# Products of zeros ahead of the maximum products of two sequences, and a plan drawn anew, in an attention and mixture-of-experts layer

## Time and profile before

| | |
|---|---|
| runs, us | 601.95, 604.53, 609.40; median 604.53 |
| the profiled execution | 607.28 us, of which the span from the first to the last instruction is 605.5 |
| mean granted clock of TensorE over the span | 0.933 |
| PE matmuls busy | 534.6 us (88%), 4350 instructions |
| DVE busy | 487.4 us (80%), 1981 instructions |
| ACT, POOL busy | 313.4 us (52%), 309.5 us (51%) |
| HBM | 64.28 MB read, 20.05 MB written |

### The profile page before, as it was taken

One profiled execution on the slowest core, in us unless ns is written; L12 is line 12 of the kernel. 1 busy time (PEld: TensorE's weight loads), 2 busy tenths in 40 slices (PEclk: granted clock), 3 DMA queues, 4 the chain that ended last, 5 costly groups with the idle time before them and its releaser, 6 DMA issues.

```text
span 605.5 us, 14722 instructions
## 1 busy us (share of the span) xinstructions
PE 534.6 (88%) x4350; PEld 355.4 (59%) x4350; DVE 487.4 (80%) x1981; ACT 313.4 (52%) x744; POOL 309.5 (51%) x517
## 2 busy tenths in 40 slices
PE   6869898979999899999999999999996977899841
PEld 3222354535656556656657777666876977885431
DVE  3797998968999889899899879879942774758883
ACT  3106945645756556567666655776661442432100
POOL 5215826555363456667874556547584423143531
PEclk9776997989999989999999899999997997999986
DMA  6483332173535445453675375643455698860111
GB/s 187 124 255 94 94 116 68 54 227 124 129 86 162 112 149 154 140 153 110 182 191 145 106 225 157 182 124 111 120 169 185 181 291 266 259 197 23 48 39 36
DMA packets 75279, 87.40 MB, mean 144 GB/s; under 512 B 9984, under 2 KB 57984, under 8 KB 75200
## 3 DMA queue, kind: packets, MB, share of 16 engines
q1 hardware_dynamic: 67984, 77.34, 43.7%
q0 software_dynamic: 3584, 7.35, 4.1%
q10 hardware_dynamic: 3632, 1.77, 1.0%
HBM read 64.28 MB, written 20.05 MB: 139 GB/s over the span
## 4 chain that ended last, share of the span: by engine, by line
PE 57%; DVE 14%; issue 10%; SPq 6%; ACT 5%; DMA 3%; another core or an unknown queue 2%; POOL 1%; ACTq 0%; DVEq 0%
PE ps L1462 15%; PE ps L1368 10%; PE ps L1324 10%; PE ps L1474 8%; DVE sums L1581 3%; PE ps L1379 3%; ACT probs L1169 2%; PE ps L1446 2%; SPq L960 2%; PE ps L1310 2%; PE ps L1484 1%; PE ps L1395 1%; DVE acc L1761 1%; PE ps L1410 1%
## 5 line engine op out<-in xcount | busy, mean ns | idle before, releaser
L1581 DVE CUSTOM_DVE_ANT_0 sums<-ps,mask_sb 128x384 bf16<-128x384 f32 (+3 forms) x512 | 218.0, 483 | 14.5 <-PE ps L1324 10.8
L1169 ACT ACTIVATE probs<-ps 128x512 f32<-128x512 f32 x320 | 170.9, 612 | 50.3 <-PE ps L1324 46.5
L1103 POOL TENSOR_SCALAR_AFFINE_SELECT probs<-probs 128x256 f32<-128x256 f32 (+1 forms) x320 | 114.2, 365 | 126.6 <-ACT probs L1169 118.8
L1324 PE MATMUL ps<-stack 64*128 64x256 bf16 (+3 forms) x1024 | 118.3, 314 | 14.5 <-DMA stack<-mparts 5.7
L1462 PE MATMUL ps<-xgT,w_tile 128*128 128x128 f32 x672 | 92.3, 284 | 3.6 <-ACT xgT L1230 2.8
L1462 PEld LDWEIGHTS ps<-xgT,w_tile 128*128 128x128 f32 x672 | 83.3, 197 | 10.7 <-issue 6.8
L1713 DVE SCALAR_TENSOR_TENSOR gate<-th,ps 128x256 f32<-128x256 f32 x116 | 48.5, 418 | 46.9 <-ACT th L1236 39.5
L1125 POOL DMA_INDIRECT yg<-rows_out,slot x56 | 54.0, 964 | 60.4 <-DVE acc L1761 33.9
L1368 PE MATMUL ps<-probs,va 128*32 128x512 f32 (+3 forms) x1024 | 81.0, 459 | 3.6 <-POOL probs L1103 1.4
L1324 PEld LDWEIGHTS ps<-stack 64*128 64x128 bf16 x1024 | 41.8, 95 | 71.5 <-issue 16.7
L1236 ACT ACTIVATE th<-ps 128x256 f32<-128x256 f32 x116 | 45.1, 390 | 52.2 <-PE ps L1462 36.6
(11 more groups left out here) (119 smaller groups left out, 707.6 us busy)
## 6 DMA issues: line engine op xcount, KB each, us to landing
w_tile<-in_experts SPq DMA_DIRECT2D x92, 384.0 KB
stack<-parts_scratch SPq DMA_DIRECT2D x98, 128.0 KB
parts_scratch<-parts SPq DMA_DIRECT2D x14, 384.0 KB
xg<-rows_in SPq DMA_DIRECT2D x18, 256.0 KB
rows_out<-y_routed SPq DMA_DIRECT2D x61, 64.0 KB
rows_in<-zeros SPq DMA_DIRECT2D x14, 192.0 KB, 3.7
x_t<-in_x SPq DMA_DIRECT2D x8, 256.0 KB
x_r<-in_x SPq DMA_DIRECT2D x8, 256.0 KB
```

The costliest lines, as they stand in the source:

```text
L1103: pool.affine_select(out=area, in_=area, compare_op=ALU.is_ge, fill=0.0, base=0, pattern=pattern, channel_multiplier=-1).then_inc(masked, 1)
L1169: act.activation(probs[:, (s * NB + v) % PRING, :], bank("scores", s, v), ACT.Exp, scale=SCALE)\
L1324: return pe.matmul(into[:, at:at + width], here[:, stationary, at_s:at_s + P], here[:, moving, at_m:at_m + width], start=True, stop=True)
L1581: ins = dve.tensor_tensor_reduce(sums[:, use % 2, at:at + w], bank("max", s, u)[:, at:at + w], mask_sb[:, S - w:S], -1.0, 3.0e38, ALU.add, ...
```

## The change

1. `max_pair`, for sequences 0 and 1: the waits for the two banks of a pair both come first; then come two rounds of products of `idle`, in each round one on rows 0 to 63 into the first bank and one on rows 64 to 127 into the second, 128 by 512; then the products of before, which overwrite the zeros. Sequences 2 to 7 issue the same instructions as before, apart from the two waits, which come first there too.
2. `length`: in the plan a pair of these two sequences takes 430 ns more.
3. All numbers in `AT` and `LATER` are drawn anew; the code that uses them is the same, and so is `COST`. "Searched under drawn delays" in the change's name says that the search for the numbers went through plans with random delays drawn into them.

```diff
-AT = dict(weight_ahead=110.3736, tables=5.4067, fill=-93.4985, fill_step=26.5143, routed0=9.7812, routed1=-2.4771,
+AT = dict(weight_ahead=76.186, tables=-17.3658, fill=-124.8669, fill_step=32.6219, routed0=9.1224, routed1=0.5053,
...
-         ("pe", "max_pair"): (-172.1, -167.21, -5.43, -127.49, -148.68, -100.62, -14.13, -12.09, -100.6, -237.59,
-         169.06, -18.79),
+         ("pe", "max_pair"): (-177.61, -128.53, 37.43, -74.99, -88.61, -59.18, 33.94, 18.05, -62.24, -216.71, 216.99,
+         -13.08),
...
+
+WARMED, WARMING = 2, 2
...
+        if kind == "max_pair" and key[0] < WARMED:
+            taken, lasts = taken + 215 * WARMING, lasts + 215 * WARMING
...
                 for pair in range(2):
                     take("max", s, 2 * w + pair)
+                for _ in range(WARMING if s < WARMED else 0):
+                    for pair in range(2):
+                        zero = idle[KS * pair:KS * pair + KS, :]
+                        pe.matmul(bank("max", s, 2 * w + pair), zero[:, 0:P], zero, start=True, stop=True)
+                for pair in range(2):
                     for k, i, at in MAX_UNITS[b]:
```

More of the change, by code:

```diff
@@ new lines @@
+AT = dict(weight_ahead=76.186, tables=-17.3658, fill=-124.8669, fill_step=32.6219, routed0=9.1224, routed1=0.5053,
+          routed2=137.2347, stay=0.5386, values=-3.6375, v=29.1374, rows1=3.9149, maxima1=-70.4109, heads_T0=-10.8792,
+          heads_T1=-180.518, out_T=38.1973, out=-125.2214, ln1_stats=23.0964, ln1=-8.2064, x1_T=46.1952,
+          router=36.0633, weights=70.8658, load_residual=69.3691, load_x=-50.3811, x_T=-71.6631, project0=-44.8146,
+          project1=-79.1125, rope=53.9864, rest=79.4813, low=-67.116, store_parts=-132.8503, stack0=-75.8479,
+          stack1=-51.451, rows0=-8.3374, maxima0=-76.2422, count=-15.9543, rank=-61.6646, scatter=128.7884,
+          scatter_step=0.115, shared=27.7133, shared_step=2.72, routed=48.9194, margin=2.3458, apart=1.2735,
+          T=-2.8221, tanh=21.694, glu=1.5347, down=-61.4607, stored=-120.3842, weight_late=14.1817, gather=-2.1911,
+          gather_step=0.7016, combine=51.1716, lull_from=-58.3092, lull_to=18.6836, lull=1.2261,
+          routed_last_but_one=1.6586, routed_last=8.7267, apart_last=0.756, gather_last=114.7465,
+          gather_step_last=1.0571, combine_last=-6.6777, dense=-1.8198, dense_step=1.3239, dense_tanh=40.0325,
+          dense_glu=98.9924, dense_down=83.4753, dense_mix=-41.9754, dense_weight=-69.8979, dense_weight_step=19.6751)
```

253 lines of the change are left out of this document (109 added, 144 removed), and 31 rows, old and new, of the table LATER.

## The result

The kernel after takes 627.12 us (median of 4 runs, 624.62 to 629.50) where the kernel before took 606.68 beside it: 1.0335 of its time, with a 95% interval of 1.0278 to 1.0392, 20.4 us more. The forecast was 599.0 us with a range up to 613. It was wrong, in the sign as well. The profiled execution of after took 629.50 us, of which the span is 627.8.

A forecast was written before the change was run, and what follows sets the result against it. DVE was taken to bound 21.2 to 44.7 us, PE at low clock 44.7 to 57, and PE's work 150 to 455. Terms 0 - 2 + 2 + 0.5 - 2 - 4 = -5.5 us gave 599.0 us against the median; range 587 to 613.

The forecast's parts named there:

- f: New places of all instructions on five queues: -4 us taken, bounded by 23.1 us of PE's idle time either way.
- Price of a round: Two added products of zeros on PE, side by side: 0.22 us at full clock; two rounds 0.44 full, 0.89 half.
- a: 21.2 to 44.7 us, DVE full: 15 pairs' zeros, 6.6 us, fit PE's 7.0 us idle, so 0; +6.4 if clock low.
- b: 44.7 to 57 us: higher clock saves 4.2 us, five pairs' zeros cost 2.2, so -2; bounds -5.6 to +4.4.
- c: 57 to 78 us, clock already 1.00: 13 pairs' zeros, 5.7 us, against 2.26 us idle PE; +2, bounds 0 to +3.4.
- d: 78 to 96.5 us: seven pairs' zeros, 3.1 us, against 2.6 us idle PE; +0.5, bounds 0 to +3.1.
- the 4 us named: Sign: the fourth transpose of maxima still stands near 96 us, within 4 us.
- e: Low-clock stretches at 97.8, 118.3 and 135.3 us, which no zeros reach: -2 us from re-placed work, bounds -8.4 to +3.4.
- D: Rival, 0.14: zeros come to about nothing; the new order moves 455 to 560 us by up to 13.2 us; 590 to 616.
- C: Rival, 0.14: zeros lengthen the path of sequences 0 and 1 on PE's queue, 21 to 96 us: +14.7, 619.2 us.
- B: Rival, 0.22: zeros keep the clock full in 43.2 to 56.8 us and three later stretches: -18.0, 586.5 us.

## Why the prediction was wrong

**The failed step is f.** The prediction put it so: "The long stretch is 97% busy, which leaves order little, so I take a sixth, -4." The order alone measures +2.7% (the kernel without zeros), 16.6 us by its ratio to the 604.53 us of the runs before the prediction, some 20 us from that -4. The bound of 23.1 us, "as much the other way", held; the choice near nothing failed. What the step left out is the wait: with indirect DMAs 1.27 us apart the other engines learned up to 15.3 us late that PE had finished, and spacing them takes 3.9 points off after, more than the 3.35 that the change cost. The argument was that a stretch with little idle time has little to lose. It has little to win; a stretch that is 97% busy can lose any amount, and from 150 to 455 us PE's idle time grew by 12.6 us, over the 8 us that the prediction had named as a sign against f. I had asked how good the new order could be for PE and not what it does to POOL's queue, though "past POOL's gathers too" stood in the step.

**The evidence was at hand.** The chain and the waits were read at the start of the kernel, since most of the low clock was there. ACT's idle time of 7.78 us with no known releaser, in the middle of nine scatters, was in the trace of before, and the chain of before has 2% of "another core or an unknown queue" with one core. The code shows it as well: `plan` keeps a least distance between indirect DMAs (`GAP, GAP_LAST, GAP_END = 2600, 1300, 0`, L225), and lets PE's work end at least 1.1 us after an indirect DMA that was issued less than 1 us before that end (`HOLD`, L226 and L724). It reads as if the late signals had been known, though no comment says so. But the distance is kept in the plan's time only. The queue that comes out of it holds scatter after scatter with nothing between, and once POOL is late they can start as fast as it issues them, 1.27 us apart. For the last group the plan even allows 1.3 us, which is no more than that pace, and takes it that PE's work comes through between two of them; the traces show that for most of a run it does not.

**The terms, one by one.**
- Price of a round, 0.22 us: right (0.44 and 0.85 us for two), though the ratio of 1.9 that I named gives 0.23. The Trainium skill (TensorE: Matmul & The Clock Gate, Part 3, "The mechanism") has weight loads run under a matmul in flight only where the row groups differ, which would have each round show its weight load; the two rounds of 0.44 us do not bear that out here either. The same section also names loads into a background weight buffer, with which 0.44 us would agree; no run here tells whether that is the way.
- a, 0: right. DVE is busy 23.12 of 23.50 us, and in the order of before the first transpose of maxima stood at 37.7 us (38.03 in the earlier trace rows).
- b, -2: right for the clock, not for the time. The first values group fell from 4.49 us to the 2.36 that was forecast; with the same order and no zeros it takes 4.21. PE of after, then of the new order without zeros:

```profile
52.78 2.36 PE L1372 MATMUL ps<-probs,va 128*32 128x512 f32 x32
...
51.69 4.21 PE L1372 MATMUL ps<-probs,va 128*32 128x512 f32 x32 [0.51 <-POOL probs L1102]
```

But the second transpose of maxima came only 0.2 us earlier for the zeros, in either order (55.97 to 55.80 us, 57.11 to 56.91). The low clock from 43 to 57 us shrank to 6.8 us, half:

Busy times of after in three stretches of low clock, the columns as above.

```profile
44.00:50.80 6.80, 6.13 (x38) 2.52 (x38) 4.86 (x15) 5.21 (x10) 4.75 (x9) 0.50 0.82 250
112.20:119.10 6.90, 6.90 (x43) 3.37 (x46) 5.76 (x32) 1.09 (x2) 2.91 (x5) 0.51 0.56 167
463.80:480.90 17.10, 6.78 (x30) 5.81 (x31) 4.74 (x23) 2.15 (x7) 7.19 (x8) 0.50 0.18 58
```

- c and d, +2.5: in the order of before they came out near their upper bounds together. The zeros moved the third transpose from 72.63 to 76.76 us and the fourth from 96.19 to 102.55, 6.4 us in all; bounds +3.4 and +3.1. That delay was made up later (a later transpose stands at 173.8 us against 173.0 of before), so it is not what the +0.9% consists of; in that kernel's own run of nine scatters ACT waits 11.3 us where before's waits 7.8, which may be part of it. In the order of after the fourth stands at 97.16 us, within the 4 us named, but DVE waits 7.3 us for maximum products from 21 to 98 us, over the 3 us by which I had said that c would be wrong.
- e, -2: too little for the clock; what it gave in time was not measured apart. Of the three low stretches from 97 to 140 us (17.1 us) one is left, 6.9 us; two had been forecast to remain.

So the clock did what it was to do, and more: of 44.4 us of low clock before 150 us 17.1 are left, and without the zeros 37.5. At half speed the 20.4 us between the two hold some 10 us of PE's time to be regained, against the 17.6 us that the zeros take at full clock. The two together measure between -0.3 and +0.9%. The new low stretch of 17.1 us at 463.8 us is no cause but a trace of the late signals: PE does 6.78 us of work there. With it and others behind 150 us, after's mean granted clock over the span is 0.935 where before's was 0.933, so the clock was won early and lost again later.
That no time came of the higher clock in the first 150 us is measured; that DVE bounds the first stretch and that the zeros took what PE had won is my reading of it, not shown apart.

**The rivals.** D (0.14) named the right half of the change and the right place, 455 to 487 us; its bound of ±13.2 us, PE's idle time there, was too small for the same reason as f. C (0.14), the only one wholly over 2% slower, has 619.2 us by the wrong mechanism: the zeros cost at most 0.9% by the four ratios, some 5.5 us, not 14.7. B (0.22) had the clock right in two of its four places, and no time came of it.

## What to carry to other kernels

The idle time of the busiest engine bounds what a new order can win, not what it can lose: go through every queue that it rewrites, and ask what now stands back to back in it. Where a plan keeps instructions apart, the queue has to do so too, by work or a wait between them; here 0.57 us of idle work for POOL between indirect DMAs brought before to 0.985 and after from 1.034 to 0.995 of before's time. And look at every wait whose releaser the profile does not know: on this one core it was a finished engine whose signal came late.

## What the hardware showed that was not expected

- While POOL issued indirect DMAs 1.27 us apart (0.97 us each and 0.30 between), readers of PE's finished products started late: by 10.8 to 15.3 us in after's run of 14, by 5.8 us in before's run of nine and 7.3 us in the same run with short instructions in it. At 1.5 us apart one such wait was still there, at 1.6 to 1.8 us none; an instruction of 0.11 us in the 0.30 us between two DMAs did not help. Why these signals are late, no run here shows: only the distance was varied, and what stands in it.
- Less low clock need not bring time: 17.1 us before 150 us against 37.5 in the same order, for times of 1.0335 and 1.0274 of before's. The products of zeros that raised the clock took time of PE themselves, so this does not show that the low clock was free.
